# Attention sweep and expert-tile loop of a fused transformer layer: tiles three deep, y normalised on ScalarE, DVE's sweep order and POOL's scatters rearranged

## What is computed

```python
x = hidden                                                 # (4, 1024, 256)
x = x + attn(layernorm(x))     # 16 heads of 16; query i sees keys i-63 .. i; softmax; Wo
z = layernorm(x)
logits = z @ gate_w.T + lb_bias
topw, topi = top_k(sigmoid(logits), 2);  topw = topw / (topw.sum(-1) + 1e-8)
for e in range(8):
    wmean = (topw * (topi == e)).sum() / count(topi == e)  # one weight per expert, over all tokens
    out += where(token chose e, (silu(z @ Wg[e].T) * (z @ Wu[e].T)) @ Wd[e].T * wmean, 0)
out += (silu(z @ Sg.T) * (z @ Su.T)) @ Sd.T
return x + out
```

## Time and profile before

| | us |
|---|---|
| median of 3 runs | 596.92 |
| lowest, highest | 594.46, 598.95 |
| profiled execution, its own time | 591.49 |
| its span, first to last instruction | 589.7 |
| PE busy in the span | 521.1 |
| DVE busy | 414.3 |
| ACT busy | 315.9 |
| POOL busy | 222.4 |

### The profile page before, as it was taken

The page is one execution under the profiler, slowest core; times in us unless marked ns, Lnnn a source line. Parts: engine busy times, 40 slices in busy tenths (PEclk is TensorE's granted clock), DMA queues, the critical chain, the costliest instruction groups (busy, mean ns, idle before and its releaser), DMA issues.

```text
span 589.7 us, 16243 instructions
## 1 busy us (share of the span) xinstructions
PE 521.1 (88%) x5573; PEld 431.5 (73%) x5573; DVE 414.3 (70%) x1299; ACT 315.9 (54%) x736; POOL 222.4 (38%) x384
## 2 busy tenths in 40 slices
PE   7699989999988998999999877888889889789997
PEld 4567777777777776787677546787788887678996
DVE  6566788788888888888887763655555665552675
ACT  3566666665765766666576422314566665653111
POOL 4000011253154145225314427622555555453651
PEclk8899999988999999998999975989999999999999
DMA  8500101212212231221112033586444444434994
GB/s 261 188 2 4 38 4 38 83 39 84 83 42 79 83 94 46 83 82 39 55 57 74 32 127 115 178 209 220 140 138 146 145 142 135 133 107 135 400 399 154
DMA packets 42751, 67.96 MB, mean 115 GB/s; under 512 B 9772, under 2 KB 28847, under 8 KB 42672
## 3 DMA queue, kind: packets, MB, share of 16 engines
q1 hardware_dynamic: 34128, 42.72, 23.3%
q0 software_dynamic: 6528, 16.86, 8.3%
q10 hardware_dynamic: 2016, 7.34, 3.6%
HBM read 36.02 MB, written 31.66 MB: 115 GB/s over the span
## 4 chain that ended last, share of the span: by engine, by line
PE 70%; DVE 19%; issue 5%; ACT 3%; another core or an unknown queue 1%; DMA 1%; SPq 0%; POOL 0%; ACTq 0%; DVEq 0%; POOLq 0%
PE ps L524 37%; PE ps L583 6%; PE ps L612 5%; PE ps L767 5%; DVE rmax L1115 4%; PE ps L837 3%; PE ps L594 3%; DVE stats L1096 2%; PE ps L620 2%; PE ps L578 2%; DVE xs L1145 2%; PE ps L599 2%; PE ps L535 2%; PE ps L854 2%; PE ps L650 2%
## 5 line engine op out<-in xcount | busy, mean ns | idle before, releaser
L524 PE MATMUL ps<-wF,wA 128*128 x648 | 106.8, 303 | 10.4 <-DVE wA L1413 7.1
L524 PEld LDWEIGHTS ps<-wF,wA 128*128 128x128 f32 x648 | 85.7, 189 | 20.3 <-issue 18.4
L509 POOL DMA_INDIRECT y_rows<-vm,dest x72 | 70.4, 978 | 79.6 <-ACT vm L1068 32.9
L1115 DVE TRANSPOSE_TENSOR_REDUCE rmax<-ps 128x32 f32<-128x1024 f32 x64 | 79.3, 1239 | 10.0 <-PE ps L583 9.9
L937 ACT ACTIVATE probs<-ps 128x1024 f32<-128x1024 f32 x64 | 65.6, 1024 | 36.0 <-PE ps L599 35.6
L413 POOL TENSOR_TENSOR rstd<-mv,epsb 128x2 f32<-128x2 f32 x32 | 6.4, 201 | 207.2 <-DVE mv L1100 206.2
L469 POOL DMA_INDIRECT z_slots<-z,slot x64 | 64.7, 1010 | 28.2 <-issue 16.9
L524 PE MATMUL ps<-yT,wA 128*128 128x256 f32 x384 | 69.2, 314 | 1.6 <-DVE yT L1090 1.5
L583 PE MATMUL ps<-bd,kT 64*128 64x256 f32 x512 | 69.9, 395 | 0.0
L524 PEld LDWEIGHTS ps<-yT,wA 128*128 128x128 f32 x384 | 55.4, 204 | 5.2 <-issue 2.9
L583 PEld LDWEIGHTS ps<-bd,kT 64*128 64x128 f32 x512 | 51.6, 198 | 5.7
(11 more groups left out here) (183 smaller groups left out, 1157.0 us busy)
## 6 DMA issues: line engine op xcount, KB each, us to landing
z<-z_slots SPq DMA_DIRECT2D x72, 129.0 KB
zT_scratch<-zT SPq DMA_DIRECT2D x16, 512.0 KB
bd<-y_rows SPq DMA_DIRECT2D x8, 512.0 KB, 10.7
out<-xs SPq DMA_DIRECT2D x16, 256.0 KB, 7.5
wraw_of<-wffn SPq DMA_DIRECT2D x10, 384.0 KB, 3.8
xs<-x SPq DMA_DIRECT2D x7, 512.0 KB, 6.6
wA<-zT_scratch ACTq DMA_DIRECT2D x7, 512.0 KB, 6.2
shift<-negs SPq DMA_DIRECT2D x128, 2.0 KB
```

Source lines behind the costliest of these rows:

```text
L509: eng.indirect_dma_start(y_rows, bass.IndirectOffsetOnAxis(ap=dest[:, m:m + 1], axis=0), yo[:, m, :], None, bounds_check=K * T - 1, oob_is ...
L524: mm = eng.matmul(out, lhsT(a), rhs(b), start=start and n == 0, stop=stop and n == 2, skip_group_check=skip)
L1115: eng.tensor_reduce(rmax[:, n % 2, 0:32], S[n % 2].rearrange("p a (c q) -> p (a c) q", q=32), AX.X, ALU.max, apply_transpose=True).then_in ...
```

## The change

Three parts. (1) In the sweep y is normalised by ACT, as Identity(rstd · x - mean · rstd), for which POOL makes minus mean times rstd; the first two groups stay on DVE. (2) DVE's and PE's order in a step changes: the statistics of z move from block 2 to block 3, one bn_stats of y to the end of block 2; single instructions move between the maxima and `neg_max`; the second half of `split_weights` moves to block 0 of the next step; PE makes zT ahead of the second half of q, and ACT reads it ahead of q. POOL issues the four scatters one at a time, the later three each once the scores of the block are there, and rstd of z comes after all four. (3) In the tile loop the distances grow to t + 3, t + 1, t - 1, t - 3, with three buffers for z1, h1, hT in place of two.

```diff
+                    if which == 0:
+                        after(eng, s_yz[0], TPG * (value - 1))
+                        eng.tensor_tensor(minus_mean[:, 0, :], mv[:, 0, :, 0], minus1[:, :], ALU.mult).then_inc(s_mm, 1)
                     eng.tensor_tensor(rstd[:, which, :], mv[:, which, :, 1], epsb[:, :], ALU.add).then_inc(s_ve[which], 1)
...
+                        eng.wait_ge(s_mm, value)
+                        eng.tensor_tensor(minus_mean[:, 1, :], minus_mean[:, 0, :], rstd[:, 0, :], ALU.mult).then_inc(s_sh, 1)
...
                         places(g - GPB, place)
-                        scatter(g - GPB, place, (0, 1))
+                        for n in range(TPG * K):
+                            if n and ahead:
+                                eng.wait_ge(s_S, BPG * g + n + 1)
+                            scatter(g - GPB, place, (n,))
...
                         rstd_of(1, g)
-                    if g >= GPB and ahead:
-                        scatter(g - GPB, place, (2, 3))
...
+                        if n == 0 and old >= 2:
+                            zT_of(g - 2, (place - 2) % GPB)
                         if project:
                             project(g + 1, (1,))
...
-                        if n == 0 and old >= 2:
-                            zT_of(g - 2, (place - 2) % GPB)
...
                 def tile(q, m, first, last):
-                    if not (last and m >= 6):
-                        rows_T(*later(q, m, 2))
+                    if not (last and m >= 5):
+                        rows_T(*later(q, m, 3))
                     if not (last and m == 7):
                         tile_gate_up(*later(q, m, 1))
...
-                    if m == 1 and not last:
+                    if m == 3 and not last:
                         experts_of(q + 1)
-                    hidden_T(*later(q, m, 0))
                     if not (first and m == 0):
-                        tile_down(*later(q, m, -1))
+                        hidden_T(*later(q, m, -1))
+                    if not (first and m < 3):
+                        tile_down(*later(q, m, -3))
...
+                def normalise_y(G):
+
+                    eng.wait_ge(s_sh, G + 1)
+                    for t in range(TPG):
+                        eng.activation(y[:, t, :], xs[:, TPG * G + t, :], ACT.Identity, bias=minus_mean[:, 1, t:t + 1],
+                                       scale=rstd[:, 0, t:t + 1]).then_inc(s_yz[0], 1)
...
+                        if n == 0 and ahead == 2:
+                            normalise_y(g + 2)
+                        if n == 0 and old >= 2:
+                            zT_hi(g - 2, old >= 3)
                         if n == 0 and ahead:
                             q_copy(g + 1)
-                        if n == 0 and old >= 2:
-                            zT_hi(g - 2, old >= 3)
...
                     eng.wait_ge(s_T, t + 1)
-                    after(eng, s_g1, t - 1)
-                    eng.copy(z1[:, m % 2, 0, :], ps[:, 4 + m % 2, 0:D]).then_inc(s_zh, 1)
+                    after(eng, s_g1, t - 2)
+                    eng.copy(z1[t % 3][:, 0, :], ps[:, 4 + m % 2, 0:D]).then_inc(s_zh, 1)
...
-                    hidden_lo(*later(q, m, 0))
-                    destinations(*later(q, m, 0))
+                    if not (first and m == 0):
+                        hidden_lo(*later(q, m, -1))
+                    if not (last and m == 7):
+                        destinations(*later(q, m, 1))
```

More of the change, by code:

```diff
@@ L1091, in lo_of, with statistics @@
                                       ALU.subtract).then_inc(s_out, 1)
-                def statistics(which, G):
-                    for t in range(TPG):
+                def statistics(which, G, first=range(TPG), last=True):
+                    for t in first:
                         eng.bn_stats(stats[:, which, t, :], xs[:, bass.ds(TPG * G + t, 1), :].rearrange("p o d -> p (o d)")
                                      ).then_inc(s_bn[which], 1)
-                    for t in range(TPG):
+                    if which == 0 and last:
+                        after(eng, s_sh, G)
+                    for t in range(TPG) if last else ():
                         wait_apart(eng, s_bn[which], TPG * G + t + 1)
@@ L1164, in link, with comparisons @@
                     eng.wait_ge(s_rk, value)
-                def comparisons(G):
+                def comparisons(G, first=True, last=True):
                     lg = logits[:, bass.ds(TPG * G, TPG), :]
@@ L1205, in step @@
                             normalise(1, g - 2, (place - 2) % GPB)
+                        if n == 1 and old == 3:
+                            comparisons(g - 3, last=False)
+                        if n == 3 and old:
+                            statistics(1, g - 1, (0,), False)
                         if ahead or n < BPG - 1:
@@ L1218, in step @@
                         if n == 1 and old == 3:
[L1219 removed]
+                            comparisons(g - 3, first=False)
                             ranks(g - 3)
@@ L1227, in step @@
                             residual(g - 1)
+                        if n == 3 and old:
+                            statistics(1, g - 1, (1,))
                         if n == 3 and g + 3 < NG:
-                            for c in range(2, XC) if old == 1 else ():
-                                eng.wait_ge(s_x[c], 16)
-                            statistics(0, g + 3)
+                            statistics(0, g + 3, (1,))
                         if n == 3 and ahead == 2:
@@ L1238, in step @@
                             oT_lo(b - 1, (n - 1) % BPG)
-                        if n == 2 and old:
-                            statistics(1, g - 1)
+                        if n == 2 and g + 3 < NG:
+                            for c in range(2, XC) if old == 1 else ():
+                                eng.wait_ge(s_x[c], 16)
+                            statistics(0, g + 3, (0,), False)
                         if n == 3 and ahead and old >= 2:
                             logits_add(g - 2)
-                        if n == 3 and 3 <= g < NW + 3:
-                            split_weights(g - 3, 1)
                 def prologue():
@@ L1443, in _ @@
                 hidden(0, 0, 0)
+                rows_lo(2, 0, 2)
+                destinations(0, 0, 0)
                 sweep_tiles(eng, tile)
+                hidden_lo(NTS - 1, NTS // 8 - 1, 7)
                 def combined(g):
```

81 lines of the change are left out of this document (49 added, 32 removed).

## The result

The changed kernel takes 623.04 us (median of 4 runs, 621.01 to 624.9) against 596.96 us (594.46 to 598.95) in the same comparison: ratio 1.0438, 95% interval 1.04 to 1.0475. The profiled execution took 622.33 us around a span of 620.2, where 591.49 and 589.7 stood before: 30.5 us more of span. The forecast was 568 us.

What follows compares the result with a forecast made beforehand. PE and DVE were taken as nearly full in the loaded sweep, and late results as stalling the tile loop. Savings of 15 us (sweep) and 14 us (tiles) from the 596.92 us median gave 568 us, range 554 to 583.

Steps and rivals of the forecast that it cites:

- Scatters one by one: Sweep: issuing POOL's four scatters singly changes nothing, 0 us, bounds -0.6 to +0.3 us a step.
- one more wait like that for oT: Sweep: upper bound for the scatters' new placement, +0.3 us a step, sized like PE's wait for oT.
- The sweep's order: Sweep: loaded step falls to 19.4 us, saving 1.3 in each of 10, 0.6 in light ones; 15 us in all.
- Rival B: Sweep is a ring of dependent stages, so relieving DVE gains only 3 us: 580 us; chance 0.12.
- y on ACT: Sweep: two activations replace DVE's work, 1.1 us a step, covered by ACT's idle time before q_copy.
- The destinations: Tile loop: dest needs an earlier scatter landed; chain of 4.5 us against 5.84 available, so no wait.
- The tile loop: Deeper order lets PE bear delays of 1.0 us instead of 0.46: 14 us saved (4 to 22), 1.64 us a tile.
- Rival A: Tile loop's late results follow POOL's scatters, so tiles gain 4 us instead of 14: 578 us; chance 0.17.
- The range: Whole kernel: 554 to 583 us, with a chance of 0.85 for faster by over 1%.
- the 0.06 for slower: Whole kernel: chance 0.06 of coming out slower, from dest waiting for its scatter in the tile loop.
- Rival D: Tile loop: dest waits for its scatter, 2.1 us a tile, so the kernel is slower at 601 us; chance 0.06.

Runs made afterwards that it cites:

- e7: Kernel before with the tile loop's 72 POOL scatters replaced by plain DMAs on SP to fixed rows: 562.7 us, 1.004 of before.
- e8: Changed kernel with the scatters in two pairs, each begun when transposed block maxima arrive, on the fast chip: 550.3 us, 0.981 of before.
- e4: Kernel before with only the deeper tile order and its third buffers: 592.4 us, 1.002 of before.
- e12: Changed kernel with the tile loop's 72 POOL scatters replaced by plain DMAs on SP to fixed rows: 597.2 us, 1.002 of before.
- e6: Kernel before plus a plain 132 KB store by SP in each of 48 blocks, POOL's scatters unchanged: 559.8 us, 0.998 of before.
- e3: Changed kernel with each later scatter waiting for the scores of one block later: 593.3 us, 1.003 of before.
- e1: Changed kernel with the four scatters back in two pairs, behind the places and behind rstd of z: 620.3 us, 1.046 of before.
- e2: Kernel before with only the edit that issues the sweep's four scatters singly: 604.8 us, 1.020 of before.
- e11: Kernel before with a second scatter of 8 bytes a row behind each of a group's four, on a chip with late results: 670.3 us, 1.125.
- e5: Kernel before with a second scatter of 8 bytes a row behind each of a group's four, on the fast chip: 582.8 us, 1.040.

## Why the prediction was wrong

**The step that failed** is "Scatters one by one": "I take 0", with bounds of -0.6 to +0.3 us a step. It measured +3.6 to +3.9 us (a block of 8.73 against 5.0) in nine of the 11 steps and +2.2 and +1.6 in the others, some 38 us in all, of which the relief in the other blocks gave back 14. Two things were wrong in it. The edit doesn't do what its words say: when the places of a group are done, the scores of two more blocks are there, so three scatters go in one row. And I counted a scatter as POOL's time and nobody's wait. On these chips, where a result of PE is due behind such a row, it reaches the other engines only 1.4 us (one or two scatters) to 2.3 us (four) after the last one has begun, and rows of 8 bytes do it too. The bound "one more wait like that for oT" came from the small waits of the trace of before, in which the pairs happened to stand where nobody waited for PE. The effect did stand in it: the late silu of the earlier trace rows and the waits of the earlier trace rows in the tile loop, which has a scatter in every tile, and the 4.2 us of "remote" in the line of pvs in the earlier trace rows. The last is two waits, each behind four scatters in a row, and the first of them is in step 15, the one step of the sweep where the kernel before issues all four at once. Here are the fourth scatter and what follows:

```profile
340.00 0.98 POOL L469 DMA_INDIRECT z_slots<-z,slot  x1 [0.30 <-issue]
...
342.12 0.37 ACT L943 COPY pvs<-ps 128x256 f32<-128x256 f32 x1 [1.84 <-remote]
342.25 0.28 DVE L1120 TENSOR_REDUCE negm<-ps 32x32 f32<-32x128 f32 x1 [2.51 <-PE ps L594]
```

That block took 8.06 us, from the maxima at 338.49 to those at 346.55; on the fast chip the same block takes 5.86 (e7). It was the price of a row of scatters in front of waited-for results, in the trace that the forecast was made from.

**The sweep's order** was right where no scatter stood: 0.6 us was forecast for the light steps, and step 2 gained 0.66. On the fast chip, with the scatters moved, the loaded step gains 1.06 us (20.73 in e7, 19.67 in e8) against a forecast of 1.3, and from the first maxima of step 1 to those of step 15 it is 14.9 us less (274.05 against 288.95), against a forecast of 15; at the first dest 9.4 of them are left (385.7 against 395.1), and where the rest went is not traced. The relief was real and was given back by the scatters. Rival B (a ring), which gave the sweep 3 us, falls with that. The forecast took one loaded step of 20.75 us for all; six of the 11 in the kernel before took 21.2 to 21.6.

**y on ACT** was right: a pair takes 1.09 us (forecast 1.1), POOL's shift is ready at 219.27 + 0.20 and y starts at 219.50, and the next instruction of ACT waits for PE, not for y.

**The destinations** were right: no wait for their scatter is named in the loop, and the landing that I had to choose between 1.58 and 3.8 us, and took as 2.5, has a median of 2.4 in e8, on the fast chip, for these very scatters (the traces of the other chips give none):

```profile
y_rows<-vm,dest POOLq DMA_INDIRECT x72, 2.4
```

**The tile loop** was mis-sized: 14 us forecast, 1.83 to 1.81 us a tile measured, and no gain in e4. Rival A had the mechanism, "the late results follow the scatters": e12 shows it, since without POOL's scatters the same loop takes 1.50 us a tile. On the fast chip the loop takes that with the scatters, in the old order too (1.51 in e6, 394.7 to 501.9), so depth had nothing to gain there. What I had taken for a delay of fixed size that more depth can bear is, in the sweep, one that grows with the row of scatters; that the tile loop's grows in the same way is argued from its longest wait, 2.8 us with the deeper order and 1.9 before. My reason against A, that ACT makes up time, only said that the row ends sometimes. It had 0.17 of the chances, and 578 us, since it left the sweep alone.

**The range** of 554 to 583 us and the 0.06 for slower had no case in which a moved scatter lengthens the sweep. Rival D had the sign, but its mechanism (a full queue behind dest) is not what happened in the changed kernel.

## What to carry to other kernels

An indirect DMA issued by GpSimd has to be placed like an instruction of every engine that waits for PE, not like one of GpSimd alone: begin a pair where the next 3 us hold no result of PE that is waited for (the second begins 1.3 to 1.4 us behind the first, and the hold ends 1.5 behind that), and check in the timeline how many go in one row. A semaphore wait spreads instructions only if it is still unfulfilled when the engine gets there. Where results come late, first find what makes them late; three buffers instead of two bought nothing here, taking the scatters off POOL bought 25 us (in a kernel that doesn't sort the rows back).

## What the runs showed of the hardware

- On three chips of four PE's results arrive late while POOL issues scatters back to back (1.27 to 1.39 us from start to start, 0.97 to 1.08 us each). Behind the start of the last scatter the waiting engine starts after 1.3 to 1.4 us for a single one (e3), 1.4 to 1.5 for two (e1), 1.6 to 1.9 for three (the changed kernel, seven steps; up to 2.1 in e2), 2.1 to 2.4 for four (e11 and step 15 of the kernel before). In the changed kernel DVE's result reached PE within 0.1 us at the same time. In the sweep of the fast chip nothing of it is seen, with two or four scatters in a row (e5 to e8), and the kernel before is 30 us faster there, 560.8 against 591.5 to 595.6. So two runs of a kernel with such DMAs can differ by 5 per cent with no difference in the code. Only one of the four chips was used in two sessions (595.6 both times), so that it is the chip and not something else of the session is likely, not shown. Why they differ, and what in POOL's issuing holds PE's results, the traces don't show.
- The pause of 2.0 us in PE was followed by a granted clock of 0.51 and six products in 1.63 us instead of 0.96, a second loss behind the first.
- A memset of 0.33 us between two scatters on POOL cost 0.80 us (2.08 against 1.28).
